# A fused two-layer block: PSUM banks, side work and the place of the weighted sums in its first attention

## The reference, cut to what matters

```python
q = (x @ Wq).reshape(b, n, N_HEADS, HEAD_DIM)
k, v = jnp.split(ctx @ Wkv, 2, axis=-1)
...
q = apply_axial_rope(q, pos_map)
k = apply_axial_rope(k, ctx_pos_map)
logits = jnp.einsum('bqhd,bkhd->bhqk', q, k) * scale
w = jax.nn.softmax(logits, axis=-1)
attn = jnp.einsum('bhqk,bkhd->bqhd', w, v)
...
return attn @ Wout + bout
```

## The kernel before, in words

| s | items | s | items |
|---|---|---|---|
| 0 | rest of O1 with the bias, k0b | 8 | rest of K1, q0a |
| 1 | X0, weighted | 9 | k0a, weighted |
| 2 | k1b, half of Q0 | 10 | V0 |
| 3 | rest of Q0, C | 11 | q1a, V1 |
| 4 | X1, K0 | 12 | k1a, a quarter of O0 |
| 5 | a quarter of Q1, weighted | 13 | a quarter of O0, weighted |
| 6 | half of Q1 | 14 | rest of O0 with the bias, q0b |
| 7 | rest of Q1, half of K1 | 15 | q1b, half of O1 |

## Time and profile before

### The profile page before, as it was taken

One profiled execution on the slowest core, in us unless ns is written; L12 is line 12 of the kernel. 1 busy time (PEld: TensorE's weight loads), 2 busy tenths in 40 slices (PEclk: granted clock), 3 DMA queues, 4 the chain that ended last, 5 costly groups with the idle time before them and its releaser, 6 DMA issues. The chain is left out here.

```text
span 2185.0 us, 37999 instructions
## 1 busy us (share of the span) xinstructions
PE 1893.5 (87%) x11294; PEld 1380.0 (63%) x11294; DVE 1127.2 (52%) x2563; ACT 921.9 (42%) x2626; POOL 1012.6 (46%) x1058
## 2 busy tenths in 40 slices
PE   4689999999879999989999999966799999765992
PEld 1355666666549899978888899953565655422441
DVE  5567767777545763322332222226677778561114
ACT  3367777776633322222222222212566666432110
POOL 1478777877510542222333343424565454155540
PEclk9999999999889999999999999988899999977996
DMA  8588888787715663579778766432444444182446
GB/s 313 179 250 261 262 250 247 227 254 237 239 48 180 113 140 87 149 216 283 210 198 233 228 163 161 88 74 85 96 99 98 92 100 110 33 231 77 138 135 259
DMA packets 189404, 373.74 MB, mean 171 GB/s; under 512 B 47658, under 2 KB 89267, under 8 KB 183380
## 3 DMA queue, kind: packets, MB, share of 16 engines
q1 hardware_dynamic: 157596, 309.18, 46.6%
q0 software_dynamic: 31616, 62.14, 13.3%
HBM read 193.42 MB, written 135.33 MB: 150 GB/s over the span
## 5 line engine op out<-in xcount | busy, mean ns | idle before, releaser
L701 ACT ACTIVATE a_P<-a_SC,a_nm 128x256 f32<-128x256 f32 x512 | 235.9, 473 | 132.2 <-DVE a_nm L606 131.4
L1174 POOL DMA_INDIRECT b_y_rows<-b_ysb,b_entry x79 | 124.6, 1577 | 351.2 <-DMA b_y_rows<-b_ysb,b_entry 227.4
L606 DVE TENSOR_REDUCE a_nm<-a_SC 128x2 f32<-128x512 f32 x256 | 164.8, 685 | 142.4 <-PE a_SC L847 142.4
L1383 DVE TENSOR_TENSOR b_xl<-b_XT,b_xh 128x512 fp32r<-128x512 f32 x111 | 76.7, 691 | 250.0 <-ACT b_xh L1325 248.9
L569 POOL TENSOR_TENSOR a_praw<-a_praw,a_phigh 128x704 f32<-128x704 f32 (+2 forms) x126 | 191.2, 1517 | 10.3
L858 PEld LDWEIGHTS a_T<-ident,a_P 128*128 128x128 f32 x1024 | 119.2, 145 | 74.6 <-issue 39.7
L858 PE MATMUL a_T<-ident,a_P 128*128 128x128 f32 x1024 | 147.2, 283 | 21.5 <-DVE a_PT L618 20.6
L567 POOL CAST a_phigh<-a_praw 128x704 fp32r<-128x704 f32 (+2 forms) x126 | 112.7, 895 | 93.8 <-DMA a_praw<-in_L_ffn_wd 32.6
L1389 DVE TENSOR_TENSOR b_al<-b_AT,b_ah 128x384 fp32r<-128x384 f32 x111 | 61.8, 557 | 176.7 <-ACT b_ah L1330 176.7
L1320 ACT ACTIVATE b_ysb<-b_Y 128x512 f32<-128x512 f32 x79 | 47.3, 598 | 249.5 <-PE b_Y L1265 249.5
L2039 ACT ACTIVATE c_P<-c_SC,c_nm 128x240 f32<-128x240 f32 x256 | 115.7, 457 | 76.9 <-DVE c_P L1931 76.8
(11 more groups left out here) (478 smaller groups left out, 4826.3 us busy)
## 6 DMA issues: line engine op xcount, KB each, us to landing
w_parts<-a_phigh SPq DMA_DIRECT2D x72, 352.0 KB, 3.5
w_parts<-a_praw SPq DMA_DIRECT2D x72, 352.0 KB, 4.2
b_wh<-w_parts SPq DMA_DIRECT2D x18, 1216.0 KB, 10.6
b_wl<-w_parts SPq DMA_DIRECT2D x18, 1216.0 KB, 13.6
c_q<-c_qT SPq DMA_DIRECT2D x64, 256.0 KB, 4.3
c_k<-c_kT SPq DMA_DIRECT2D x128, 128.0 KB
b_wh<-w_parts SPq DMA_DIRECT2D x18, 704.0 KB, 5.2
b_wl<-w_parts SPq DMA_DIRECT2D x18, 704.0 KB, 8.1
```

Of the source, the lines that this page charges most:

```text
L606: eng.tensor_reduce(nm[:, g % 4, j, :], SC[j][:, :].rearrange("p (t k) -> p t k", t=BT), AX.X, ALU.max, negate=True).then_inc(topped, 1)
L701: e = eng.activation(Pr[:, i, t, :], SC[j][:, t * S:(t + 1) * S], ACT.Exp, bias=nm[:, g % 4, j, t:t + 1], accum_out=den[:, h, t:t + 1])
L1174: eng.indirect_dma_start(out=y_rows, out_offset=bass.IndirectOffsetOnAxis(ap=entry[:, r, 1:2].bitcast(U32), axis=0), in_=ysb[:, v % RING, ...
```

## The change: banks, order, instruction sizes and rows of the bias

`W` has two banks and `SC` three. Head j of pair g uses bank (2g + j) mod 3, so that `scores(g)` waits for the exponentials of head 0 of g - 1 and of head 1 of g - 2. The weighted sums are issued behind `scores(s + 2)`; the turned reciprocals stay where they were. GpSimd's casts and subtractions of a piece are issued in parts of 176 columns, with one semaphore increment by the last of each. `ones` and `bias` have 128 rows, of which all but two are zero, set by two more memsets at GpSimd's start.

```diff
-    NW_ = 3
+    NW_, NS_ = 2, 3
...
-    SPLIT_AT, NRAW, NHIGH = -6, 4, 3
+    SPLIT_AT, NRAW, NHIGH, SHORT = -6, 4, 3, 176
...
-        brow, blow, bias = sb("brow", [1, D]), sb("blow", [1, D], F32R), sb("bias", [2, D], F32R)
-        one, ones = sb("one", [2, P]), sb("ones", [2, P], F32R)
+        brow, blow, bias = sb("brow", [1, D]), sb("blow", [1, D], F32R), sb("bias", [P, D], F32R)
+        one, ones = sb("one", [2, P]), sb("ones", [P, P], F32R)
...
-        SC = [ctx.enter_context(nc.psum_tensor(f"a_SC{i}", [P, 512], F32)) for i in range(2)]
+        SC = [ctx.enter_context(nc.psum_tensor(f"a_SC{i}", [P, 512], F32)) for i in range(NS_)]
...
+            eng.memset(r32(ones[:, :]), 0.0).then_inc(rows_zero, 1)
+            eng.memset(r32(bias[:, :]), 0.0).then_inc(rows_zero, 1)
...
-                eng.tensor_copy(high[:, 0:k * m], raw[:, 0:k * m]).then_inc(phigh_done, 1)
+                parts = [slice(a, min(a + SHORT, k * m)) for a in range(0, k * m, SHORT)]
+                for c in parts:
+                    o = eng.tensor_copy(high[:, c], raw[:, c])
+                o.then_inc(phigh_done, 1)
                 eng.wait_ge(phigh_done, i + 1)
-                eng.tensor_tensor(raw[:, 0:k * m], raw[:, 0:k * m], r32(high[:, 0:k * m]),
-                                  ALU.subtract).then_inc(plow_done, 1)
+                for c in parts:
+                    o = eng.tensor_tensor(raw[:, c], raw[:, c], r32(high[:, c]), ALU.subtract)
+                o.then_inc(plow_done, 1)
...
-            eng.tensor_copy(ones[:, :], one[:, :]).then_inc(bias_set, 1)
+            eng.wait_ge(rows_zero, 2)
+            eng.tensor_copy(ones[0:2, :], one[:, :]).then_inc(bias_set, 1)
...
-                for j in range(2):
-                    ge(eng, exp_done[j], g)
+                ge(eng, exp_done[0], g)
+                ge(eng, exp_done[1], g - 1)
...
-                            m = eng.matmul(SC[j][:, t * S:(t + 1) * S], q[r:r + R, p // 2, t * P:(t + 1) * P],
+                            m = eng.matmul(SC[(2 * g + j) % NS_][:, t * S:(t + 1) * S], q[r:r + R, p // 2, t * P:(t + 1) * P],
...
+            def turn_reciprocals(n):
+
+                ge(eng, att_ready, n)
+                eng.wait_ge(rec_wide, n + 1)
+                for t in range(BT):
+                    eng.transpose(O[:, S + t * P:S + (t + 1) * P],
+                                  recw[:, n % 2, t, :, :].rearrange("p h e -> p (h e)"), core.ident[:, :])
...
                 if s % SLOTS == 1 and SLOTS < s <= END + 1:
-                    weighted((s - SLOTS - 1) // SLOTS)
+                    turn_reciprocals((s - SLOTS - 1) // SLOTS)
                 if 0 <= s < END:
                     turn_exponentials(s)
                 if 0 <= s + LEAD < END:
                     scores(s + LEAD)
+                if s % SLOTS == 1 and SLOTS < s <= END + 1:
+                    weighted((s - SLOTS - 1) // SLOTS)
```

More of the change, by code:

```diff
@@ L403, in rope_attention @@
         wq_ready, all_scales = sem("wq_ready"), sem("all_scales")
-        consts, vseq = sem("consts"), sem("vseq")
+        consts, vseq, rows_zero = sem("consts"), sem("vseq"), sem("rows_zero")
         ctx_loaded, xn_ready = sem("ctx_loaded"), sem("xn_ready")
@@ L605, in top @@
                 eng.wait_ge(scored[j], g + 1)
-                eng.tensor_reduce(nm[:, g % 4, j, :], SC[j][:, :].rearrange("p (t k) -> p t k", t=BT),
+                eng.tensor_reduce(nm[:, g % 4, j, :], SC[(2 * g + j) % NS_][:, :].rearrange("p (t k) -> p t k", t=BT),
                                   AX.X, ALU.max, negate=True).then_inc(topped, 1)
@@ L700, in exponentials @@
                 for t in range(BT):
-                    e = eng.activation(Pr[:, i, t, :], SC[j][:, t * S:(t + 1) * S], ACT.Exp, bias=nm[:, g % 4, j, t:t + 1],
+                    e = eng.activation(Pr[:, i, t, :], SC[(2 * g + j) % NS_][:, t * S:(t + 1) * S], ACT.Exp, bias=nm[:, g % 4, j, t:t + 1],
                                        accum_out=den[:, h, t:t + 1])
@@ L867, in weighted @@
                     is_freed(eng, (b, "V1"))
-                ge(eng, att_ready, n)
-                eng.wait_ge(rec_wide, n + 1)
                 for j in range(2):
                     eng.wait_ge(pt_done[j], SLOTS * (n + 1))
-                for t in range(BT):
-                    eng.transpose(O[:, S + t * P:S + (t + 1) * P],
-                                  recw[:, n % 2, t, :, :].rearrange("p h e -> p (h e)"), core.ident[:, :])
                 for k in range(BT):
```

## The result

The changed kernel takes **2214.0 us** (median of 9 runs, 2206.7 to 2223.2) where the kernel before takes 2190.2 on the same chip (9 runs, 2185.3 to 2235.4): ratio 1.0095, 95% interval 1.0074 to 1.0115. The forecast was 2203 (own range 2188 to 2220) from a kernel before at 2194, so +9 and no difference to be measured; it is +24: under 2%, yet its interval leaves out no change. The median lies in the forecast's own range, in part by the 7 us added for new runs, of which 3.4 came (2190.2 for 2186.8). The profiled execution has a span of 2221.4 us (time 2223.15), 36.4 over that of before.

A forecast was written before the change was run, and what follows sets the result against it. TensorE's own work was taken to set the pace. The terms -3.7 + 0.6 + 15 - 3 - 3.5 + 1 + 2.5 + 0 - 1.5 + 2 gave +9.4 us, 2196, plus 7 for new runs: 2203 us, range 2176 to 2230.

The forecast's parts named there:

- the price of GpSimd's short instructions: GpSimd's casts and subtractions: 0.12 us an added instruction, mostly swallowed by its load waits; +1 us, first batch +2.5.
- Rival C: GpSimd becomes the bound beyond 0.19 us an added instruction; `widened` and rotations set the pace; 2224 us median; chance 0.17.
- Everything else together: All terms besides GpSimd's short instructions: -3.7 + 0.6 + 15 - 3 - 3.5 + 0 - 1.5 + 2.
- Weighted sums behind scores: Transposes of steps 1, 9 stall 0.87 us, of 5, 13 0.39 us; 2.5 us a batch, 15 us.
- the 3 us that were to come back in steps 7 and 11: Stalls from VectorE's lateness shrink, 0.6 to 0.4 and 0.4 to 0.1 us; 0.5 us a batch.
- E: End of the previous scores; in step 44 the second four transposes start 2.11 us after it, the scores 2.88.
- Third bank: Scores wait for head 0 alone; steps 6, 8, 10, 12 win 3.7 us in the middle, batch 0 some 1.5.
- the first chain: VectorE's two maxima, then its copy, before the second four transposes at E + 2.11; scores then at E + 2.67.
- Two projection banks: An item waits for the eviction of n - 2 instead of n - 3; 0.1 us a batch, +0.6 us.
- End: At the stage's end the moved sums hold up copies and transposes of steps 118 and 122; +2 us in all.
- rival D: Four 0.4 to 0.9 us stalls a batch lower TensorE's clock; at least 1 us a batch, +7; chance 0.08.
- Rival B: Moved sums let VectorE and ScalarE run ahead, E + 2.11 seldom met; -15 us, 2179 as a median; chance 0.30.

The follow-up runs named there:

- f1: The changed kernel with GpSimd's casts and subtractions whole again: 66.86 us a batch, stage end 651.5, ratio 1.0055 to the kernel before.
- e1: The kernel before with three score banks and two for projections alone: 65.83 us a batch, stage end 640.7, ratio 0.9997.
- e4: The kernel before with the bias over 128 rows alone: 65.70 us a batch, stage end 644.6, ratio 1.0007.

## Why the prediction was wrong, and where it was right

**The step that failed is the price of GpSimd's short instructions: "these waits swallow most of it", +1 us in the middle and +2.5 in the first batches, measured +18.9 (f1 to changed).** Its input was right: 0.12 us an added instruction was forecast, 0.14 came (a cast and a subtraction of 704 columns took 0.77 and 1.68 us, now 1.16 and 2.11), and GpSimd's busy time in a batch went from 50.5 to 62.0 us, where 60 was forecast. The Trainium skill (GPSIMD Engine Reference, 3.1 Elementwise, side-by-side cycle accounting) gives about 2.6 cycles an element for two inputs and a software dispatch besides, without a time for it. The estimate that the prediction worked out from this, 0.16 us an instruction, is as near to the trace's 0.14 as the 0.12 taken. The swallowing was right too as far as it went: of the 11.5 us added to a batch, the waits of GpSimd took 8.3 (15.5 to 7.2 us) and 3.2 came out. What I did not read is **where** the waits lie: 3.0 of the 40 us with the rotations and 11.5 of the 26 behind, in the lines shown above, which the trace of before had. The rotations came 1.3 to 2.9 us later, as forecast ("1 to 3 us"); "`high_part` holds ScalarE; behind the sums it mostly has that time" is the sentence that fell. In the kernel before ScalarE had already stood 26.6 us for rotations in the stage, 0.42 of it in one step of the batch above, so it had little to give:

```profile
257.01 0.63 ACT L736 ACTIVATE a_hlk<-a_rot 128x512 fp32r<-128x512 f32 x1 [0.42 <-POOL a_rot L548]
```

By stretch: GpSimd's part was 6.3 us in the first two batches (forecast 2.7), 11.7 in the five of the middle (0.8), 0.9 at the end. In the middle it lies in steps 6 (0.90 us a batch over f1), 10 (0.44), 11 (0.32), 8 (0.25), 7 (0.17), 5 (0.15) and 9 (0.11) and in no other.

Rival C named the engine and the size but not the way. It had GpSimd become the bound at 0.19 us an instruction with `widened` late; at 0.14 it has slack left in every batch, and `widened` held TensorE 1.3 us in all between 168 and 576 us. In the first batches C's wait is real, 9.80 us before the first reciprocals (5.06 us of item and wait together in step 5 before, 10.93 after, 7.46 in f1, so 3.5 by the short instructions):

```profile
127.08 0.69 PE L874 MATMUL a_O<-ident,a_recw 128*128 128x128 f32 x2 [9.80 <-POOL a_recw L557]
```

**Everything else together was forecast at +5.9 us and measured +8.6 (f1's stage).** In the middle it was 4.5 forecast (five sixths of 15 - 3.7 + 0.6 - 3 - 3.5) and 4.3 measured; in the first two batches -0.6 forecast and +3.1 measured, at the end +2 and +1.2. The agreement in the middle is partly luck: the bias, priced at nothing, gave 0.69 us a batch (steps 0 and 14), while step 7, which was to lose 0.2 us, became 0.18 longer (f1 over before).

- *Weighted sums behind scores.* The gaps are right in mechanism, place and size; the 3 us that were to come back in steps 7 and 11 did not (+0.18 and -0.18 us a batch). TensorE in step 45 (13 mod 16) of the changed kernel:

```profile
300.61 0.38 PE L874 MATMUL a_O<-ident,a_recw 128*128 128x128 f32 x2
300.83 0.60 PE L865 MATMUL a_T<-ident,a_P 128*128 128x128 f32 x4
301.79 0.41 PE L865 MATMUL a_T<-ident,a_P 128*128 128x128 f32 x2 [0.36 <-DVE a_PT L625]
```

  E is 299.65 and the second four transposes start at 301.79, E + 2.14 against 2.11. From reciprocals to scores this step takes 1.73 us (0.22 + 1.51) where 1.33 would do, 0.40 lost for 0.39 forecast; the steps of 1 mod 16 take 2.21, 0.88 for 0.87. From step 32 to 112 these two are alike in every batch (the whole step 3.36 or 3.37 us); in steps 5 and 9 the wait for GpSimd's rotation or widening sometimes stands ahead (3.51 and 3.47 in the mean, 3.36 in f1).
- *Third bank.* Right that it moves little (e1: -2.3 us of stage; forecast -3.7 and -1.5), for the first chain lies just below.
- *Two projection banks.* +0.6 forecast; between 168 and 576 us products waited 1.1 us in all for evictions, 4 times.
- *Bias.* Priced at zero, since "a product's length goes by its columns"; its record went from 0.50 to 0.80 us at the same 512 columns, and yet the step with it became 0.35 us shorter (4.47 to 4.12), 16 times. e4 alone gives most of it back in steps 6 and 7 (+0.24 and +0.41 us a batch). Whole time can't show it.
- *End.* +2 forecast, +2.2 measured (84.0 to 86.2 us from scores(112) on), but 0.9 of it is the short instructions' (f1: 85.2). The sums there took 3.43 us against 3.33, and the next transposes wait for ScalarE's copy:

```profile
613.24 3.43 PE L890 MATMUL a_O<-a_PT,a_V 128*32 128x256 f32 x32
617.54 1.06 PE L865 MATMUL a_T<-ident,a_P 128*128 128x128 f32 x8 [0.88 <-ACT a_PT L715]
```

- *Clock (rival D).* The middle stood at 0.98 instead of 1.00, in two places: 0.70 from 168 to 185 us and 0.90 from 406 to 423. The steps that lie in them are 3.0 us longer than f1's in the first two batches (steps 16 to 18) and 1.3 in the middle (72 and 73), what they waited included; it is not in every batch as D had it. What spoke against D was a rounding: the 1.00 of the earlier trace rows hides some 3.5 us at the lower of the clock's two levels, right behind the 1.23 us stall of step 103. That stretch of the kernel before, TensorE's busy time and count, then clock, DMA share and GB/s:

```profile
529.40:532.90 3.50, 3.50 (x12) 0.51 0.83 288
```

- *Rival B* fell: steps of 1 and 13 mod 16 have their gap in every batch.

What stays open: of the 18.9 us `widened` has 3.5 in step 5 and 1.3 in the middle. The rest of the middle, 10.4 us, lies in the steps behind the high parts and their normalise and maxima, and how it divides between the high parts' wait, that chain and the clock behind them no run separates; nor the rest of the first two batches.

## What to carry to other kernels

Slack has a place. Before a busy engine is given more work, split the period at the points where others wait for it and read its idle time in each piece; a wait for loads behind the last deadline is worth nothing to the deadlines. And in an in-order queue look for an instruction that needs nothing of the waiting one ahead of it: moving `low_part` past `normalise` was worth 14 us of stage, where the best of the four parts of this change gained 2.

## What the runs showed of the hardware

- **A product with 2 rows of stationary data costs more than one with 128**, though its own record is shorter (0.50 against 0.80 us). The weight loads show why, before and then in e4_bias, the last load of `a_wo` and that of the bias:

```profile
291.04 0.19 PEld L793 LDWEIGHTS a_W<-a_wo,a_aT 128*128 128x128 f32 x1 [0.24 <-issue]
291.99 0.18 PEld L798 LDWEIGHTS a_W<-a_bias,a_ones 2*128 2x128 f32 x1 [0.76 <-issue]
```

```profile
294.10 0.19 PEld L796 LDWEIGHTS a_W<-a_wo,a_aT 128*128 128x128 f32 x1 [0.24 <-issue]
294.53 0.19 PEld L801 LDWEIGHTS a_W<-a_bias,a_ones 128*128 128x128 f32 x1 [0.24 <-issue]
```

  Two rows are loaded 0.95 us after the load before, 128 rows 0.43 us: the 2-row load started 0.07 us ahead of the end of the product in flight (292.06), the 128-row load 0.59 ahead of it (295.12).
- **Short GpSimd instructions back to back** start every 0.277 us (cast) and 0.516 us (subtraction) at 176 columns. A cast of 704 columns behind the indirect DMA takes 1.34 us instead of 0.77 whole, and 1.73 instead of 1.16 in four parts in the median (2.13 at 265.21 above).
- **VectorE's `low_part`** took 1.10 us in the mean and takes 0.87 beside short instructions; the forecast was 0.75. Its wait for GpSimd can be read off: in the kernel before each of the 26 low parts that began with 0.18 us or more left of a GpSimd cast, addition or subtraction took that rest + 0.55 us, all others 0.66 to 0.69. Here 1.32 us were left, and it took 1.87. Shortening the wait was worth less than its price.

```profile
523.65 1.67 POOL L569 TENSOR_TENSOR a_praw<-a_praw,a_phigh 128x704 f32<-128x704 f32 x1
```

```profile
524.00 1.87 DVE L641 TENSOR_TENSOR a_hlk<-a_rot,a_hlk 128x512 f32<-128x512 f32 x1
```
